# Four-layer transformer kernel on one core: the first layer's routing rows and router products placed elsewhere in a batch, with the products as 32-column tiles

## The reference

```python
x = x + tanh(g_xattn[0]) * L0_xattn(layernorm(x), ctx, ...)   # q k v, softmax, relu(out @ W1 + b1) @ W2 + b2
x = x + tanh(g_ffn[0])   * L0_ffn(layernorm(x), router_w, router_b, w1, w2)
    # logits = rows @ router_w + router_b    (256 x 8)
    # route = softmax(logits); the row goes to argmax and its result is multiplied by max(route)
x = x + tanh(g_xattn[1]) * L1_xattn(layernorm(x), ctx, ctx, ...)
x = x + tanh(g_ffn[1])   * L1_ffn(layernorm(x), w_gate, w_up, w_down)   # ternary weights, 8-bit rows
```

## Time and profile before

| | us |
|---|---|
| median of 3 runs | 624.98 |
| lowest, highest | 622.17, 625.14 |
| the profiled execution | 620.89 |
| its span from first to last instruction | 619.1 |
| TensorE busy in it | 502.2 (81%) |
| VectorE busy | 382.0 (62%) |
| ScalarE busy | 259.9 (42%) |
| GpSimd busy | 252.9 (41%) |
| mean granted TensorE clock, share of full speed | 0.904 |

### The profile page before, as it was taken

How to read it: one execution, slowest core, us unless ns; L and a number is a source line. 1 busy time by engine, 2 the same in 40 slices (tenths; PEclk the granted TensorE clock), 3 DMA queues, 4 the chain that set the end, 5 groups by cost and what they waited for, 6 DMA issues and landing times.

```text
span 619.1 us, 10659 instructions
## 1 busy us (share of the span) xinstructions
PE 502.2 (81%) x3557; PEld 393.8 (64%) x3558; DVE 382.0 (62%) x782; ACT 259.9 (42%) x441; POOL 252.9 (41%) x322
## 2 busy tenths in 40 slices
PE   4767988888794399999999999939487877558994
PEld 2443846657684199999999999924355544335552
DVE  4387888797834644342424422225879998868993
ACT  1234746344460054342433332311354454526884
POOL 3364234254400252020101010037245868737996
PEclk9967989999596589999999999975689899697999
DMA  7930010000055134933465210013000000000101
GB/s 209 298 119 1 1 35 2 34 1 1 34 203 201 54 127 133 332 118 103 153 228 180 74 32 19 17 51 94 1 0 1 2 0 1 1 1 0 35 34 68
DMA packets 28631, 46.38 MB, mean 75 GB/s; under 512 B 2380, under 2 KB 24920, under 8 KB 26552
## 3 DMA queue, kind: packets, MB, share of 16 engines
q1 hardware_dynamic: 24328, 39.02, 18.8%
q0 software_dynamic: 1680, 4.59, 2.5%
q10 hardware_dynamic: 2592, 2.36, 1.1%
HBM read 38.36 MB, written 7.60 MB: 74 GB/s over the span
## 4 chain that ended last, share of the span: by engine, by line
PE 48%; DVE 30%; issue 7%; POOL 6%; ACT 4%; DMA 3%; ACTq 0%; DVEq 0%; SPq 0%; POOLq 0%
PE bank L917 20%; PE bank L929 7%; DVE s_max L1363 5%; DVE p_sum L1381 5%; DVE probs L1371 4%; PE bank L662 4%; PE bank L778 3%; PE bank L995 3%; DVE stats L1296 2%; DVE ew L1318 2%; DVE xn L1318 2%; ACT probs L1062 2%; DVE x_res L1510 1%; PE bank L632 1%; PE bank L633 1%
## 5 line engine op out<-in xcount | busy, mean ns | idle before, releaser
L917 PE MATMUL bank<-q_t,ew 128*128 128x128 f32 x1152 | 136.7, 277 | 1.4 <-DVE probs_t L1639 1.0
L917 PEld LDWEIGHTS bank<-q_t,ew 128*128 128x128 f32 x1152 | 132.8, 193 | 3.1 <-DVE probs_t L1639 2.0
L470 POOL TENSOR_TENSOR probs<-probs,p_rcp 128x1024 f32<-128x1024 f32 x32 | 61.0, 1908 | 109.7 <-DVE p_rcp L1384 109.7
L1639 DVE TENSOR_TENSOR probs_t<-bank,probs 128x512 f32<-128x512 f32 x36 | 24.8, 690 | 78.4 <-ACT probs L1184 78.4
L690 PE MATMUL bank<-ident,probs 128*128 128x128 f32 x256 | 41.4, 314 | 31.7 <-POOL probs L470 28.9
L690 PEld LDWEIGHTS bank<-ident,probs 128*128 128x128 f32 x256 | 33.8, 162 | 43.8 <-POOL probs L470 33.3
L529 POOL TENSOR_TENSOR token_now<-token_of,carried 128x1 uint32<-128x1 uint32 x17 | 4.9, 286 | 126.9 <-PE bank L903 126.8
L1062 ACT ACTIVATE probs<-probs 128x1024 f32<-128x1024 f32 x32 | 33.9, 1058 | 51.9 <-DVE probs L1371 51.9
L1092 ACT COPY probs_t<-bank 128x512 f32<-128x512 f32 x64 | 35.0, 588 | 45.1 <-PE bank L690 45.0
L1363 DVE TENSOR_REDUCE s_max<-bank 128x8 f32<-128x512 f32 x64 | 40.4, 672 | 15.4 <-PE bank L675 15.2
L1184 ACT ACTIVATE probs<-bank 128x512 f32<-128x512 f32 x36 | 21.5, 599 | 62.8 <-PE bank L917 62.8
(11 more groups left out here) (207 smaller groups left out, 1095.7 us busy)
## 6 DMA issues: line engine op xcount, KB each, us to landing
ew<-in_L_ffn_w SPq DMA_DIRECT2D x8, 2048.0 KB
ew<-in_L_ffn_w SPq DMA_DIRECT2D x8, 1024.0 KB, 5.9
slots_y<-xn ACTq DMA_DIRECT2D x18, 128.0 KB, 2.0
x_res<-in_x SPq DMA_DIRECT2D x4, 512.0 KB, 6.8
token_rows<-ew SPq DMA_DIRECT2D x4, 512.0 KB, 3.0
out_rows<-x_res SPq DMA_DIRECT2D x3, 512.0 KB, 2.9
w<-in_L_xattn_W SPq DMA_DIRECT2D x2, 512.0 KB, 8.6
ew<-in_L_ffn_w_gate SPq DMA_DIRECT2D x1, 1024.0 KB, 9.0
```

The lines of the kernel that those rows point to most:

```text
L470: nc.gpsimd.tensor_tensor(p, p, p_rcp[:, i, :].unsqueeze(2).to_broadcast([P, H, M]), ALU.mult).then_inc(s["p_norm"], 1)
L917: last = nc.tensor.matmul(o[:, P * j:P * j + P], ew1[:, s, k, c0:c0 + P], xs_t[:, par, k, :], start=(k == 0), stop=(k == DK - 1))
```

## The change

Four things, all in layer 0's attention.

- `router_turn(b-1)` goes from ahead of `values(0)` to behind `queries`. Behind it comes `scores(b+1, 0)`, which until now followed `turn(2)`; then `router_columns(b-1)`, then `turn(2)`, `router_turn_back(b-1)`, `weight_sum(b)` and `turn(3)`. The waits for the logits and the weight mean go from `queries` half 1 to `values(1)`.
- For batches 0 to 2 the products are now `router_columns`: the router's weights, widened with zeros to 32 columns (`rw_wide`), are the stationary operand and the 128 rows of a tile stream through, each tile into its own 32 partitions of one bank. ScalarE copies the 128 x 128 result (`logit_t`), TensorE turns it back, and VectorE adds the bias. Batch 3 keeps `router_products`.
- ScalarE's `router_rows` and the new copy go behind its `queries`; VectorE's `weight_scale` and `router_logits` go behind its scores of batch b+1's tile 0.
- VectorE fills `rw_wide` (a memset and a copy) behind the two `bo` instructions, each counted on `v_bo`, and TensorE waits for `v_bo` to reach 4 before `attention(0, 0)`.

```diff
-        sum_out = x_bank[1][:, 2 * P + TB * E:2 * P + TB * E + 1]
+        logit_t_out = x_bank[1][:, 2 * P:3 * P]
+        logit_turned = x_bank[0][:, 2 * P:3 * P]
+        sum_out = x_bank[0][:, 3 * P:3 * P + 1]
...
# TensorE, queries
                 for m in range(DK):
-                    if l == 0 and m == 1 and not start:
-                        pe.wait_ge(v_wm, n)
-                        if not first:
-                            pe.wait_ge(r_lg, n - 1)
...
# TensorE, between() of values(0)
-                    if l == 0 and not first_batch:
-                        router_products(b - 1)
-                    if l == 0 and not last_batch:
-                        weight_sum(b)
                     if not last_batch:
                         turn_rows(l, b + 1)
...
                 pe.wait_ge(s["a_pt"], TB * b + 2)
-                if l == 0 and not first_batch:
-                    router_turn(b - 1)
                 values(0)
                 if not last_batch:
                     queries(l, b + 1, first_batch, False)
 
+                if l == 0 and not first_batch:
+                    router_turn(b - 1)
+                if l == 0 and not last_batch:
+                    scores(l, b + 1, 0)
                 if l == 0 and last_batch:
                     ternary_chunk(0)
                     ternary_chunk(1)
+                if l == 0 and last_batch:
+                    pe.wait_ge(v_olo, 2 * DK * b + DK)
+                if l == 0 and not first_batch:
+                    router_columns(b - 1)
                 turn(2)
...
-                if not last_batch:
+                if l == 0 and not first_batch:
+                    router_turn_back(b - 1)
+                if l == 0 and not last_batch:
+                    weight_sum(b)
+                if l == 1 and not last_batch:
                     scores(l, b + 1, 0)
                 turn(3)
...
-                    pe.wait_ge(r_lg, B - 1)
+                if l == 0 and not first_batch:
+                    pe.wait_ge(r_lg, b)
+                if l == 0 and not last_batch:
+                    pe.wait_ge(v_wm, b + 1)
                 values(1)
...
+            def router_columns(b):
+
+                pe.wait_ge(r_e, 3 * b + DK)
+                for k in range(DK):
+                    for j in range(TB):
+                        last = nc.tensor.matmul(logit_t_out[32 * j:32 * j + 32, :], rw_wide[:, k, :],
+                                                xn_t[:, k, P * j:P * j + P], start=(k == 0), stop=(k == DK - 1))
+                last.then_inc(r_l, 1)
...
             pe.wait_ge(d_rout, 16 * 7)
+            pe.wait_ge(v_bo, 4)
             attention(0, 0, True, False)
...
# VectorE, scores
-                if i >= 2:
+                if i >= 2 or following:
                     dve.wait_ge(s["t_pt"], 2 * g - 2)
...
                 nc.vector.tensor_scalar(bo[l][:], bo[l][:], tg[:, l:l + 1], None, ALU.mult).then_inc(v_bo, 1)
+            nc.vector.memset(rw_wide[:], 0.0).then_inc(v_bo, 1)
+            dve.wait_ge(v_bo, 3)
+            nc.vector.tensor_copy(rw_wide[:, :, 0:E], rw[:]).then_inc(v_bo, 1)
...
```

More of the change, by code:

```diff
@@ L344, in _ @@
             expert_first(1, 1)
[L345 removed]
+            sp.wait_ge(r_l, 2 * B - 1)
             sp.wait_ge(d_rows, 16 * B)
@@ L1110, in attention @@
                 turned(1)
-                if l == 0 and not first_batch:
-                    router_rows(b - 1)
                 exps(l, b, 2)
@@ L1115, in attention @@
                 if not last_batch:
-                    if l == 0 and not first_batch:
-                        act.wait_ge(r_l, b)
                     turned_rows(l, b + 1)
@@ L1473, in attention @@
                     lower_outputs(0, 1)
-                if l == 0 and not last_batch:
-                    weight_scale(b)
-                if l == 0 and not first_batch:
-                    router_logits(b - 1)
                 if not last_batch:
@@ L1488, in attention @@
                 if not last_batch:
-                    scores(l, b + 1, 0)
+                    scores(l, b + 1, 0, l == 0)
+                if l == 0 and not first_batch:
+                    dve.wait_ge(r_l, 2 * b)
+                if l == 0 and not last_batch:
+                    weight_scale(b)
+                if l == 0 and not first_batch:
+                    router_logits(b - 1, logit_turned)
+                if not last_batch:
                     if l == 0:
```

31 lines of the change are left out of this document (20 added, 11 removed).

## The result

| | before | after |
|---|---|---|
| median of 6 runs each, same chip, us | 623.88 | 631.38 |
| lowest, highest | 621.83, 627.76 | 629.30, 632.55 |
| the profiled execution, us | 620.89 | 629.30 |
| its span | 619.1 | 627.5 |
| mean granted clock in it | 0.904 | 0.893 |

The ratio is 1.0112, with a 95% interval of 1.0074 to 1.0151: slower by 4.6 to 9.4 us. A ratio here is estimated from all fast runs of both kernels, so it differs a little from the quotient of the two medians. The two profiled executions differ by 8.4 us. To see where, I follow one instruction through the batches: the first product of `W2` on TensorE, which every batch has once, late in it.

A forecast was written before the change was run, and what follows sets the result against it. VectorE was taken to set the start, with the chain then changing hands and batch ends going through GpSimd's bias. 4.1 + 2 x 0.5 + 0 = +5.1 on a 624.98 median gave 630.1 us, range 626.3 to 634.0.

The forecast's parts named there:

- Batch 0, +4.1: Layer 0's start: TensorE's wait for v_bo 4 delays first turn and scores, and batch 0 ends 4.1 us later.
- Batches 1 and 2, +0.5 each: Layer 0's middle batches: longer TensorE idle time drops the clock at the queries, costing 0.5 us per batch.
- About 0 at full clock: Batches 1 and 2 without clock loss: TensorE's lateness cancels VectorE's 0.58 gain; about 0 us each, bounds -0.6 and +0.4.
- The three small instructions behind the subtraction, 0: VectorE, batches 1 and 2: moved instructions cost nothing under the wait for GpSimd if tile 0's subtraction ends before about 97.9.
- The columns: TensorE's router columns ahead of turn(2) in batches 1 and 2: taken as 0.5 us, bounds 0.3 and 1.95.
- Batch 3, 0 with a risk of +1 to +3: Layer 0's last batch: no loss, but about +1 to +3 us if the half clock lasts longer.
- Behind it, 0: Closing products, experts and layer 1 keep their order: 0 us.
- The cheaper start: Rival, 22%: TensorE catches up after batch 0's start and batches 1 and 2 each gain 0.58; +1.9 us, 626.9.
- The faster case: Rival, 5%: TensorE's routing-row waits in batches 1 and 2 are the real price, start wait hidden; about -3 us, 622.
- That the wait does nothing: Rival, 3%: v_bo is full earlier than read, so only the batches count; 625.7 us.
- The clock stays low: Rival, 20%: turns don't raise TensorE's clock, so layer 0's queries run at half clock; +8.9 us, 633.9.
- its largest term, 1.7 in batch 0: Low-clock rival's term: batch 0's queries take 6.26 us, so TensorE, not GpSimd, sets its end, +1.7 more.

The follow-up runs named there:

- e2: Kernel before, with only a TensorE wait for v_bo 2 (both bo instructions) ahead of batch 0; median 629.49 us, ratio 1.0062 to before.
- e7: Changed kernel plus 16 unread products of ones in TensorE's idle stretch ahead of batches 1 and 2's queries; median 631.49 us, ratio 1.0094 to before.
- e4: Changed kernel plus 34 turns of ones in TensorE's idle stretch ahead of the queries of batches 1 and 2; one run, 633.93 us.
- e13: As e10, but with 14 instead of 24 products of ones in the first group; median 626.58 us, ratio 1.0033 to before.
- e1: Changed kernel with TensorE's wait for v_bo moved from ahead of batch 0 to behind it; median 628.25 us, ratio 1.0066 to before.
- e5: Changed kernel with the old router products in the columns' place, without the logits' copy and turn back; one run, 641.18 us.
- e8: Changed kernel, v_bo wait behind batch 0, batch 0 in old order, 16 filling products, turns ahead of columns and turn back; median 627.40 us, ratio 1.0032.
- e11: Mended change (batches 1 and 2 as e8, batch 3 as changed kernel) plus the three product groups of e10; median 629.06 us, ratio 1.0049 to before.
- e9: Kernel before plus unread products of ones: 24 ahead of the last router turn, 30 behind the last expert tile; median 619.25 us, ratio 0.9882.
- e10: As e9, plus 10 more products of ones between layer 1's v products and its first turn; median 627.93 us, ratio 1.0068 to before.
- e12: As e9, with 40 instead of 30 products of ones behind the last expert tile; median 615.90 us, ratio 0.9873 to before.

## Why the prediction was right, and where it wasn't

The forecast was 630.1, the median came to 631.4; the sum of the steps was +5.1, and the medians differ by 7.5, the profiled executions by 8.4. That the forecast lies only 1.3 off is part luck: I put the sum on a median of 624.98 from three runs, which with six became 623.88. Step by step:

- **Batch 0, +4.1.** Measured +4.13, and each link as predicted: `v_bo` full at 45.50 (45.85 said), first turn at 45.77 (45.9), maxima at 49.52 (49.8), `xn` ended at 67.27 (67.5), next maxima at 61.89 (61.9), not passed on. e2 shows that the wait alone does it. The agreement to 0.03 us is luck: the execution began 0.26 early, and behind `xn`, 3.85 later than before, `h_lo` lost another 0.28, 0.18 of it waiting for ScalarE's exps. Memset and copy took 0.31 from the start of the one to the end of the other, at the low end of 0.3 to 0.6.
- **Batches 1 and 2, +0.5 each.** Measured +1.79 and +1.18. The mechanism was the one named, idle time of 5.8 us and the queries behind it at half clock; the term was mis-sized. The step that was off is "The first half of the queries then takes up to 3.1 (half of 6.26) instead of 1.85", of which I let 0.6 come through: I let the clock return in the middle of the queries, as the earlier trace rows show it at 90 to 91, and put whole queries at half clock second, at +1.3. They were nearly whole: 6.31 and 5.77. e7 priced it at 1.55 and 0.94. I had tied the return in the earlier trace rows to the gap of 2.43 us; the clock was in fact full behind that gap and up to 87, went down there, at the start of the queries (87.49), and came back in the window of 90 to 91. Here it went down at 90, 1.5 us before they started, and came back only at 97.
- **"About 0 at full clock".** e7 has +0.24, inside the bounds of -0.6 and +0.4, but by another road than I wrote. I let TensorE's lateness arrive through ScalarE's rounding of the second quarter. The rows show it at `p_sum`: ScalarE's exps of the next batch's first tile stand behind its rounding of `values(1)`, so they came late, and VectorE waited 0.53 for them. In the kernel before it went on at once, right behind the `o_lo` of the earlier trace rows:

```profile
100.81 1.20 DVE L1381 TENSOR_REDUCE p_sum<-probs 128x16 f32<-128x1024 f32 x1
```

- **The three small instructions behind the subtraction, 0.** Right, but not for my reason. I gave them GpSimd's cover up to 97.9, and in the changed kernel GpSimd's bias was over at 100.28 + 2.36 = 102.64, a microsecond before `xn` started. VectorE then waited for ScalarE all the same, 0.30 at `o_lo` and 0.53 at `p_sum`, so in this execution they still cost nothing. I also left out that VectorE's subtraction now waits for `turn(2)` (the `or following` of the diff), 0.30 in batch 1, under the same cover.
- **The columns**, 0.5 with bounds 0.3 and 1.95: 0.57 from the first to the next instruction (99.74 to 100.31). The estimate that the prediction took from the Trainium skill, "TensorE: Matmul & The Clock Gate", section "Part 3: Packing small matmuls", 0.8, was too long. `turn(3)` came 4.35 after the end of the queries for 2.75, 1.6 later, of which 1.0 is the router's turn.
- **Batch 3, 0 with a risk of +1 to +3.** Measured +0.43; the clock stayed at half until 178 to 179.
- **Behind it, 0.** Measured about +0.9 between 187 and the end: 0.24 up to layer 1's v products (423.34 for 415.57), the rest in layer 1. I haven't followed it up.

**The rivals.** The cheaper start fell (batch 0 gave the whole 4.1). The faster case fell by the row of the queries: they are released by `o_lo`, as before, and start 4.07 later (91.56 for 87.49), no sooner. That the wait does nothing fell with the first row. "The clock stays low" was half right. Its +1.3 for batches 1 and 2 and 0.5 in batch 3 fit the trace (1.79, 1.18, 0.43) better than the forecast, and e4 speaks for its premise that turns don't hold the clock up. But its largest term, 1.7 in batch 0, didn't come, because behind a turn and four scores from 45.77 on the clock was back by 49 to 50 (0.96 in that window) and the queries of batch 0 took 1.96 and 1.99. The same turn and scores had left the clock at half at 33 to 37 before, where 1.81 us of idle time followed and not the next turn at once; why it rose here, no run shows. The truth lay between the forecast and this rival.

**A caution on all clock terms.** They come from one profiled execution per kernel, and the clock doesn't fall at the same place in each. e13's layer 0 is word for word that of the kernel before, but in its execution the clock was at half from 86 to 95, the queries of batch 1 took 5.02 from 93.08 on, and the distances were 38.02 and 38.62:

```profile
86.00:95.00 9.00, 9.00 (x41) 0.50 0.10 35
```

So some executions of the kernel before lose 1 to 2 us per batch too, and the 1.55 and 0.94 are what the clock cost in this execution of the changed kernel, not what the change adds on average. The new order does meet it more often, though: in the three executions with it and no filling (the changed kernel, e1, e5) the queries of batches 1 and 2 took 5.63 to 6.31 all six times, while in the six executions of the old order only three of twelve distances were over 37 (e2's first, e13's two). By the ratio the change without the new wait costs about 4.1 us (e1), of which e1's own batch 0 makes 1.3; the rest, some 2.8, is about the sum of batches 1 to 3 in its trace (1.44, 1.04, 0.38).

## What to carry to other kernels

Before an instruction is put on a semaphore that a far-ahead engine must wait for, ask what that engine does next for the one that sets the end: here the wait for two instructions of 0.3 us in all cost 4.1, because they stand behind a stretch of VectorE that TensorE had no need to wait for. It is the place of the wait that costs, not the two instructions (e2, which waits only for `bo`, loses 3.98), and moving it one call down (e1) takes most of it back. When steps are moved between two instructions that hand over to another engine, count the cover they gave: scores and turns in alternation hid 0.8 us of ScalarE each, in a row they hid none. And an idle stretch of TensorE can have a second price behind it, the fallen clock: price the work behind it at half clock, or fill it with products that end just before the awaited event, and look at several batches and executions, since the filling did not hold the clock each time.

## What the runs showed of the hardware

- Unread products were worth more than the whole change under study: 54 float32 products of ones in two idle stretches took 1.2% off the kernel before (0.9882), 64 took 1.3% (0.9873), which the intervals don't tell apart, with the router's turn at 1.06 for 1.94 and queries at 3.70 for 5.85.
- With about equal time filled (3.93 and 3.84 us) and an idle gap of 2.1 to 2.2 us, the clock fell within the queries in both batches filled with 34 turns (e4) and in one of six filled with 16 products (e7, e8, e11). Behind 30 products it held over a gap of 0.21 us (e9) and fell after one of 1.67 (e13). A turn of 128 x 128 took 0.115 us, a float32 product of that size 0.23.
- Eight products of 32-column form with 128 moving columns, two accumulated per strip, took 0.65 us; eight with an 8-column moving operand took 1.95.
- ScalarE took up work 9.2 us late in e10, with its input ready and no releaser in the profile, and with the ten added products of TensorE moved from behind the v products to ahead of them (e12) it was gone. In e13, with the ten in e10's place and ten fewer in the first group, it was not there either. No run tells why.
